# One block for the whole layer: rows normalised inside the attention, shared weights split in its last batch, first shared products in its last head

## The reference, cut to what matters

```
x                         (4, 1024, 512) float32: 4 batches of 1024 rows, width 512
qkv   = x @ w_qkv         16 heads of 128 for q, k and v
probs = softmax(q k^T / sqrt(128))
value = einsum('bhqk,bhkd->bhkd', probs, v)     # = v * (column sums of probs)
x     = layernorm(x + value @ w_o)
...
scores = sigmoid(x @ router_w.T); sc = scores + e_bias
# 8 groups of 4 experts, the 3 best groups by their two best, then the 4 best experts
w      = scores of those 4, normalised, x 2.5
# per expert 160 slots of ... tokens in order of arrival (capacity 1.25 * T * 4 / 32 = 640)
out[token] += w * (silu(x W_gate[e]) * (x W_up[e])) W_down[e]
shared = silu(x shared_gate.T) * (x shared_up.T) @ shared_down.T      # inner width 512
x      = layernorm(x + out + shared)
```

## Time and profile before

| what | value |
|---|---|
| median of 3 runs | 2881.0 us (2876.99 to 2883.53) |
| the profiled execution: its own time | 2872.05 us |
| its span in the trace | 2870.3 us |
| mean granted TensorE clock | 0.976 |
| PE busy | 2761.8 us, 96% |
| DVE busy | 2209.1 us, 77% |
| ACT, POOL busy | 1358.2 and 710.2 us, 47% and 25% |
| DMA | 203.14 MB, mean 71 GB/s |

### The profile page before, as it was taken

How to read it: one execution, slowest core, us unless ns; L and a number is a source line. 1 busy time by engine, 2 the same in 40 slices (tenths; PEclk the granted TensorE clock), 3 DMA queues, 4 the chain that set the end, 5 groups by cost and what they waited for, 6 DMA issues and landing times. The chain is left out here.

```text
span 2870.3 us, 42196 instructions
## 1 busy us (share of the span) xinstructions
PE 2761.8 (96%) x12832; PEld 2290.3 (80%) x12832; DVE 2209.1 (77%) x3407; ACT 1358.2 (47%) x2305; POOL 710.2 (25%) x623
## 2 busy tenths in 40 slices
PE   8999999999999999999999999999997888799998
PEld 6888888888888888888888888888875766688876
DVE  5888888888888888888888888888886876233346
ACT  4555555555555555555555555545542221144434
POOL 1122121222221121212121211111101355466620
PEclk9999999999999999999999999999997888899999
DMA  3111111121111111211111020110005430378953
GB/s 114 37 38 33 37 33 40 33 95 33 37 39 34 33 33 62 66 37 33 36 33 40 29 92 30 32 37 29 29 8 174 136 104 30 93 235 246 263 157 132
DMA packets 222007, 203.14 MB, mean 71 GB/s; under 512 B 18861, under 2 KB 170493, under 8 KB 221937
## 3 DMA queue, kind: packets, MB, share of 16 engines
q1 hardware_dynamic: 207600, 191.04, 20.9%
q0 software_dynamic: 14336, 11.23, 2.3%
HBM read 167.90 MB, written 44.21 MB: 74 GB/s over the span
## 5 line engine op out<-in xcount | busy, mean ns | idle before, releaser
L540 PE MATMUL p_g<-xt,w_sb 128*128 (+1 forms) x4608 | 1109.1, 390 | 9.6 <-DVE xt L505 9.6
L540 PEld LDWEIGHTS p_g<-xt,w_sb 128*128 128x128 f32 x4608 | 866.6, 188 | 190.3 <-DVE xt L505 10.2
L359 ACT ACTIVATE y_even<-p_s,neg_max 128x1024 f32<-128x1024 f32 x512 | 572.7, 1119 | 941.5 <-DVE neg_max L415 941.4
L415 DVE TENSOR_REDUCE neg_max<-p_s 128x1 f32<-128x1024 f32 x512 | 625.9, 1222 | 290.5 <-PE p_s L555 286.9
L555 PE MATMUL p_s<-qk 128*128 128x512 f32 x3072 | 781.0, 390 | 7.3 <-ACT y_even L359 7.3
L555 PEld LDWEIGHTS p_s<-qk 128*128 128x128 f32 x3072 | 576.9, 188 | 129.5 <-ACT y_even L359 6.5
L430 DVE SCALAR_TENSOR_TENSOR colsum<-y_even,inv,colsum 128x1024 f32<-128x1024 f32 x448 | 579.6, 1294 | 18.5
L265 POOL TENSOR_TENSOR w_sb<-w_raw,w_sb 128x512 fp32r<-128x512 f32 x192 | 257.0, 1339 | 1268.3 <-ACT w_sb L313 1268.3
L578 PE MATMUL p_o<-wo_sb,val 128*128 128x512 f32 x1536 | 374.0, 393 | 3.4 <-DVE val L458 3.2
L578 PEld LDWEIGHTS p_o<-wo_sb,val 128*128 128x128 f32 x1536 | 288.4, 189 | 69.5 <-DVE y_sb L465 5.4
L1722 PE MATMUL p_f<-x_parts,s_sb 128*128 128x512 f32 x768 | 196.3, 416 | 5.9 <-DVE arena L1490 3.4
(11 more groups left out here) (162 smaller groups left out, 2255.1 us busy)
## 6 DMA issues: line engine op xcount, KB each, us to landing
w_raw<-in_w_qkv SPq DMA_DIRECT2D x192, 256.0 KB, 2.9
wo_raw<-in_w_o SPq DMA_DIRECT2D x64, 256.0 KB, 2.8
y_sb<-in_x SPq DMA_DIRECT2D x32, 256.0 KB, 3.6
y_rows<-y_sb SPq DMA_DIRECT2D x32, 256.0 KB, 2.1
raw_own<-in_w_gate SPq DMA_DIRECT2D x16, 512.0 KB
raw_own<-in_w_up SPq DMA_DIRECT2D x16, 512.0 KB
raw_own<-in_w_down SPq DMA_DIRECT2D x16, 512.0 KB
arena<-in_w_gate SPq DMA_DIRECT2D x16, 512.0 KB
```

What stands on the lines that cost most here:

```text
L359: act.activation(ex[:, t % 2], p_s[:, t % 2], ACT.Exp, bias=neg_max[:, t % 2], accum_out=rowsum[:, t % 2]).then_inc(act_e, 1)
L415: dve.tensor_reduce(neg_max[:, t % 2], p_s[:, t % 2], AX_X, ALU.max, negate=True)\
L540: ins = pe.matmul(p_g[:, g % 2], w_sb[:, a, r, c], xt_part(batch_par, b, c, half * NB, NB), start=(c == 0 and (a, b) == PASSES[0]), stop=( ...
```

## The change

It puts both blocks into one (`layer`), with one PSUM tensor `banks` cut up for both stages and SBUF buffers used again (the shared gate and up weights `s_gu` lie in one half of the transposed x `xt`, the transposed turns `parts` in the other). The order that is written out in each engine's `pair` and behind it changes so:

- In batches 1, 2 and 3 (counted from 0) the rows of the batch before are normalised in place in `y_sb`: the first 512 in the second head of the batch's first pair, the others in the first head of its second (`finished`). DVE does the statistics (`read_x`, L1023) in tiles 1 to 4 and the scale (`scale_x`, L1026 to L1032) in tile 5, ACT writes in tiles 6 and 7, SP's `swap` moves to the second pair and stores to `x2` (and the odd turn to `acc`) in place of `y`. The first two pairs of every batch are unrolled for it on DVE, ACT, POOL and SP.
- In the last batch SP loads eight pieces of the shared gate and up weights where x pieces came before (`load_gu`); ACT and POOL split them as they did x.
- In the last head PE transposes turn 0 (rows read back from `x2`) and does 18 of the first 24 gate/up products; behind it gate/up groups of turn 0 stand between and around the last `spread` and the out tiles.
- Turns 0 to 5 are read back from `x2` normalised; only turns 6 and 7 are normalised behind the attention. The router's and the shared down weights are loaded once the last out tile is done, the bias, the constants and the empty table at the kernel's start.
- Three scatters are under way in place of two. `hot` is kept in bf16, `chosen` goes, and `count` sums the four choices on PE: 56 matmuls of 32 columns in place of 14.
- `down` does three of the four chunks for all four tiles, then the fourth for all; before, tiles 0 and 1 were finished before 2 and 3 began.
- Weights of experts 1 and 0 are loaded before the routing's turns 1 on, of 2 after the store of turn 4, of 3 after that of turn 7.

```
         def pair(i):                                    # DVE
...
                     if t >= 1:
                         add_tile(n, t - 1)
+                    if 1 <= t <= 5 and finished(i, s) is not None:
+                        if t <= TT:
+                            read_x(finished(i, s), t - 1)
+                        else:
+                            scale_x(finished(i, s))
+                    if is_last(i) and s == 1 and t in (1, 3):
+                        lo_t(0, t - 1)
+                        lo_t(0, t)
...
+    def finished(i, s):
+        if isinstance(i, int) and i >= PB and (i % PB, s) in ((0, 1), (1, 0)):
+            return 2 * (i // PB - 1) + i % PB
+        return None
...
         def pair(i):                                    # ACT
...
                     exp_tile(n, t)
+                    if t >= 6 and finished(i, s) is not None:
+                        write_x(finished(i, s), range(2 * t - 12, 2 * t - 10))
+                    if is_last(i) and s == 1 and t in (0, 2):
+                        hi_t(0, t)
+                        hi_t(0, t + 1)
...
         def pair(i):                                    # PE
...
+                    if is_last(i) and (s, t) in ((0, 7), (1, 1)):
+                        turn(0, 2 * s)
+                        turn(0, 2 * s + 1)
+                    if is_last(i) and s == 1 and 3 <= t <= 5:
+                        gate_up(0, 0, range(6 * (t - 3), 6 * (t - 2)))
...
         pair(PAIRS - 1)
+        gate_up(0, 0, range(18, 24))
+        gate_up(0, 1)
         pe.wait_ge(dve_y, T * (PAIRS - 1))
         spread(M - 1)
+        gate_up(0, 2)
         pe.wait_ge(dve_v, 2 * M)
         for j in range(T):
             if j in (4, 5):
                 pe.wait_ge(dve_y, T * (PAIRS - 1) + j - 1)
             out_tile(PAIRS, j)
+        gate_up(0, 3)
+        turn(1, 0)
+        turn(1, 1)
+        logits(0)
...
         def swap(b, s):                                 # SP
-            for j in range(4 * s, 4 * s + 4):
-                on_sp.wait_ge(dve_y, (b * PB - 1) * T + j + 1)
-                store_y(b - 1, j)
+            for j in range(TT * s, TT * s + TT):
+                on_sp.wait_ge(act_ln, T * (b - 1) + j + 1)
+                sp.dma_start(x2_rows[:, b - 1, j], y_sb[:, j]).then_inc(out_y[j], 16)
+                if s == 1:
+                    sp.dma_start(acc_rows[:, b - 1, j], y_sb[:, j]).then_inc(out_y[j], 16)
...
                 for k in range(TOPK):                   # POOL
-                    on_pool.wait_ge(out_t[k % 2], 16 * ((TT * TOPK * c + TOPK * j + k) // 2))
+                    i = (c * TT + j) * TOPK + k
+                    on_pool.wait_ge(out_t[i % UNDER_WAY], 16 * (i // UNDER_WAY))
...
         def weigh(c):                                   # DVE
...
-            for q in range(2):
-                on_dve.wait_ge(out_t[q], 16 * TT * TOPK // 2 * (c - 1))
+            for q in range(UNDER_WAY):
+                on_dve.wait_ge(out_t[q], 16 * scattered(q, TT * TOPK * max(c - 1, 0)))
...
-            ro.then(dve.tensor_reduce(chosen[:], hot[:].rearrange("p t k e -> p t e k"), AX_X, ALU.max))
...
         def count(c):                                   # PE
...
             for j in range(TT + 1):
                 to = p_c[:, j * E:j * E + E]
-                for i in range(min(j, TT)):
-                    ins = pe.matmul(to, every[:], chosen[:, i], start=(i == 0), stop=(j == TT and i == TT - 1))
-                if j < TT:
-                    ins = pe.matmul(to, before[:], chosen[:, j], start=(j == 0), stop=True)
+                terms = [(every, i, k) for i in range(min(j, TT)) for k in range(TOPK)]
+                if j < TT:
+                    terms += [(before, j, k) for k in range(TOPK)]
+                for n, (mask, i, k) in enumerate(terms):
+                    ins = pe.matmul(to, mask[:], hot[:, i, k], start=(n == 0), stop=(n == len(terms) - 1))
...
-        def down_first(n):
+        def down(n):
             if n == 0:
                 on_pe.wait_ge(pool_s, 2)
             on_pe.wait_ge(dve_h, IC * (n + 1) - 1)
-            down(0, range(IC - 1))
-            down(1, range(IC - 1))
-            on_pe.wait_ge(dve_h, IC * (n + 1))
-            down(0, [IC - 1])
-            down(1, [IC - 1])
-        def down_second():
-            down(2, range(IC))
-            down(3, range(IC))
+            for j in range(TT):
+                if j == 2:
+                    on_pe.wait_ge(dve_f, IC * (n + 1))
+                down_part(j, range(IC - 1))
+            on_pe.wait_ge(dve_h, IC * (n + 1))
+            for j in range(TT):
+                down_part(j, [IC - 1])
```

More of the change, by code:

```diff
@@ L735, in last_norm, with layer @@
 def last_norm(nc, acc, out):
-    norm1 = KEPT.pop()
-    with norm1.stack:
-        after_attention(nc, norm1, acc, out)
-def after_attention(nc, norm1, acc, out):
-    y, router_wT, e_bias, shared_w, x2, table = norm1.routing
-    weights, C_SLOTS = norm1.experts
-    N, D = y.shape
+    calls = KEPT.pop()
+    with calls.stack as ctx:
+        layer(nc, ctx, calls, acc, out)
+def layer(nc, ctx, calls, acc, out):
+    x, xT, w_qkv, w_o = calls.attention
+    router_wT, e_bias, shared_w, x2, table = calls.routing
+    weights, C_SLOTS = calls.experts
+    B, S, D = x.shape
+    DH = 128
+    H = w_o.shape[0] // DH
+    M = B * H
+    C = D // P
+    T = S // P
+    HALVES = S // NB
+    PAIRS = M // 2
+    PB = H // 2
+    SCALE = float(DH) ** -0.5
+    Q, K, V = range(3)
+    G = 3 * HALVES
+    assert T == 8 and HALVES == 2 and PB == T and C == 4
+    N = B * S
     E = router_wT.shape[1]
@@ L1873, in _ @@
[L1873 to L1878 removed]
+            for i in of:
+                r, k, (a, b) = i // (KC * len(PASSES)), i // len(PASSES) % KC, PASSES[i % len(PASSES)]
+                at = slice(r * I + f * P, r * I + f * P + P)
+                ins = pe.matmul(p_f(f % 2, r), s_gu[:, a, k, at], parts[:, PARTS_OF[u], b, k],
+                                start=(k == 0 and (a, b) == PASSES[0]),
+                                stop=(k == KC - 1 and (a, b) == PASSES[-1]))
@@ new lines, in _ @@
+        gate_up(3, 0)
+        count(5)
+        turn(7, 0)
+        turn(7, 1)
+        gate_up(3, 1)
+        turn(7, 2)
+        turn(7, 3)
+        gate_up(3, 2)
+        count(6)
+        logits(7)
+        gate_up(3, 3)
+        down(3)
+        gate_up(4, 0)
+        count(7)
+        for f in range(1, IC):
+            gate_up(4, f)
+        down(4)
+        on_pe.wait_ge(dve_e, TURNS)
+        transposes(0)
+        transposes(1)
+        expert_gate_up(0)
+        for e in range(E):
+            if e + 2 < E:
+                transposes(e + 2)
+            if e + 1 < E:
+                expert_gate_up(e + 1)
+            if e == E - 2:
+                turn(1, 0, True)
+                turn(1, 1, True)
+            if e == E - 1:
+                turn(1, 2, True)
+                turn(1, 3, True)
+            expert_down(e)
@@ L1882 @@
+        gate_up(5, 0)
+        turn(3, 0, True)
+        turn(3, 1, True)
+        gate_up(5, 1)
+        gate_up(5, 2)
+        turn(3, 2, True)
+        turn(3, 3, True)
+        gate_up(5, 3)
+        down(5)
+        gate_up(6, 0)
+        turn(5, 0, True)
+        turn(5, 1, True)
+        gate_up(6, 1)
+        gate_up(6, 2)
+        turn(5, 2, True)
+        turn(5, 3, True)
+        gate_up(6, 3)
+        down(6)
+        for f in range(IC):
+            gate_up(7, f)
+        down(7)
 N_EXPERTS_FACTOR = (5, 4)
```

2855 lines of the change are left out of this document (1367 added, 1488 removed).

## The result

The changed kernel took 2935.43 us (median of 4, 2930.76 to 2938.12) against 2879.99 of the kernel before: a ratio of 1.019, 95% interval 1.017 to 1.021. Slower by 55 us, where 2832 was forecast. The profiled execution spans 2936.4 us.

What follows compares the result with a forecast made beforehand. PE, busy 96% of the span, was taken as the bound, with the experts waiting behind the last scatter. 12 - 15.7 + 8 - 57 + 4 = -49 from 2872 gives 2823, plus 9: 2832 us, range 2805 to 2862.

Steps and rivals of the forecast that it cites:

- A: Attention, batches 2 to 4: normalising rows there makes DVE late at PE's out tiles, 4.1 us a batch, +12 us.
- B: Seam between attention and routing: turn 0's work fills PE's waits, first scatter at 2233 instead of 2248.71, -15.7 us.
- C: Routing's scatters: three under way, 1.28 us apart, 182 us in all instead of 239, -57 us.
- D: From the last scatter to the experts, 11.9 us before: same code, 0.
- E: Late part: `down`'s new chunk order makes DVE's additions begin 2.8 us later, two other downs 0.65 each, +4 us.
- Same code: 0: Last scatter to experts (11.9 us) and the experts' 253 us: taken as unchanged, since the code is the same.
- the routing must keep up: Routing: PE has some 177 us of work until 2430, scatters end at 2435; close, and scatters decide.
- R4: Routing, slower: PE at a low clock becomes the bound, 2898 us at clock 0.6; chance 0.05.
- The closing sentence of the prediction: Routing: the forecast is wrong if scatters wait for DVE turn by turn, since then the routing, not POOL, is the chain.
- The clock's +8: Seam: at clock 0.75, 48 us of work takes 16 more; 0 if filled waits lift the clock; half taken.
- R1: Scatters: the third slot buys nothing, pitch stays 1.42 us, +19 us, 2851 us; chance 0.20.
- The stalls that I kept for transfers: Scatters: about 7.5 MB of transfers left, at 2.5 us a MB, hold them up 19 us.

Runs made afterwards that it cites:

- e5: The changed kernel, unedited, measured again on another chip: 2877.87 us.
- e6: The changed kernel with the 64-byte tile `token` allocated ahead of `xt` instead of behind it: 2844.40 us, ratio to the kernel before 0.9877.
- e17: The changed kernel, unedited, again on a different chip, as marker of that job's chip: 2878.76 us.
- e7: e6 with `down` in its former order of tiles: 2837.24 us.
- e8: The kernel before with three scatters under way in place of two: 2865.65 us against 2876.70.
- e3: The kernel before with an unused 64-byte tile put behind `xt`: 2917.40 us against 2878.05.
- e1: The changed kernel with an unused 64-byte tile ahead of `ident`, moving `w_sb` away from `xt`: 2883.07 us.
- e12: e7 with a tile of 512 bytes ahead of `ident`, so that `w_sb` moves and `xt` stays: 2833.51 us (one run).
- e14: e7 with a tile of 256 bytes ahead of `ident`, on the chip with the slow stretches: 2906.16 us (one run).
- e13: The changed kernel, unedited, a third time, on a chip that showed the slow stretches: 2945.88 us.
- e11: The changed kernel, unedited, a second time, on a different chip: 2879.33 us.

## Why the prediction was wrong

The kernel came out slower where faster was forecast, and 73 us above the range's upper end. Point by point, by its own steps, in us against the kernel before (traces; the changed kernel in e5, so without the stretches, and the same with its buffers placed well, e6):

| step of the sum | forecast | measured |
|---|---|---|
| pitch of the matmuls | not seen | +38.8 (first scatter of e5 - e6) |
| A, normalisation in the attention | +12 | +22.8 (last `project`, e6) |
| B and clock, seam | -15.7 + 8 = -7.7 | -8.1 (first scatter +14.7, less 22.8) |
| C, scatters | -57 | -53.5 (185.6, not 239.1); +3.5 in the first measurement |
| D, to the first expert | 0 | -0.0 |
| experts | 0 | +6.0 (e5), -0.6 (e17), +2.6 in the first measurement |
| E, late part | +4 | +3.6 (e5), +7.7 (e17 and the first measurement), of it 2.9 behind the last matmul and 1.2 in two waits |

**The step that failed first is one that wasn't there.** "Same code: 0" was taken for granted of every instruction that the diff only moved to other buffers. I read the change as work that is added, removed or moved in time, and not as the new memory layout that comes with putting both blocks into one. Over the attention's 9472 matmuls the 39 us are 4.1 ns each, 4.6 in the steady windows. With the buffers placed well, on a chip without the stretches, the changed kernel takes 2844.40 (e6), within the stated range and 12 above the forecast.

**The second is C's clause "the routing must keep up".** It does, on three chips: with POOL waiting once. On the fourth and in the first measurement it doesn't, and that is the largest single miss: +3.5 us for the scatters where -57 was forecast. Not because DVE or PE have too much to do, the rival that I wrote as R4 (PE the bound, at a low clock, 2898): the clock did fall, to 0.80 and in the stretch to 0.59, but in e5, with the same work and no standstill, it is 1.00 in that stretch. The closing sentence of the prediction named the sign, scatters waiting for DVE turn by turn. What stands behind it, instructions that start late while scatters run, was nowhere among the rivals, and why they start late stays open.

**A was undersized.** The waits were found where forecast, at the out tiles, 1.0 and 3.7 us a batch (e6; 0.7 and 3.4 at the slower pitch of e5) where 1.2 and 2.9 stood: 14.1 us for 12. What was left out is what follows: after the longer wait PE's next 12 matmuls take 1.5 to 2.6 us more, at a lower clock, 5.7 us in all. The last 3 of the 22.8 aren't accounted for.

**B was right in its sum, and in its terms less so.** PE's first hold in the last head was 5.94 (6.4 forecast), the second 5.33 (2.7). The clock's +8 was half of a full term, taken because nothing decided between the two ends; in e6 the granted clock is 1.00 from 2190 to 2230 and 0.66 from 2230 to 2250, where it was 0.74 to 0.77 from 2180 to 2240 before. That the halves met at -8.1 is in part luck. (The lowest 20-us slice before was 0.74, not 0.75; it changes nothing.)

**C as a rate was right**: 1.27 apart, 184 to 186 us for all (182 forecast), so rival R1 is out. The stalls that I kept for transfers are there: 22.1 us of waiting for scatters in e5, where 19 were forecast. The Trainium skill ("DMA: Bandwidth & Descriptors", "Queues, rings and completion order") says that each DMA engine takes its queues in turn, packet by packet. That scatters would then hardly be held up was my inference from it, and the 22.1 us don't agree with the inference.

**D and E** came as forecast in what the change does: E with 2.9 us behind the last matmul (3 forecast) and two waits of 0.62 (0.65 each), all of which the former order of `down` takes back (e7). The rest of the late part isn't E's. A wait of PE ahead of turn 3's second transposes was 2.2 us in the kernel before, 2.7 in e5 and 5.0 in the first measurement, and with three scatters in the kernel before (e8) 6.9; so the +3.6 of e5 is a lucky agreement.

## What to carry to other kernels

A kernel that is laid out anew in memory is a new kernel for its matmuls: before any argument on order, count matmuls per 100 us in a stretch that hasn't changed, before and after, and if the pitch moved, move the buffers against each other until it is back. Here a tile of 64 bytes was enough, both to slow a kernel (e3) and to mend one (e6).

Time a kernel on more than one chip before a verdict of 2%. And a wait of PE costs more than itself: what it does for the next microseconds, at a lower clock, is part of the price.

## What the runs showed of the hardware that was not expected

- Where the buffers of the moving operand and of the weights of `project`'s matmuls (128x512, 4-byte operands) lie 64 or 128 bytes past a multiple of 2048 bytes from each other, the attention's matmuls start 230.7 to 231.3 ns apart on average (e1, e3, the changed kernel), at a distance of 0, 256 or 512 past it 226.8 (e6, e12, e14); the granted clock is 1.00 in both. The slower pace lasts for some 7 to 11 matmuls into groups whose own operands lie well.
- On one of five chips (e13 and e14; not in e1, e5, e11 and e17), and in the first measurement, while three scatters were kept under way and POOL issued one each 1.27 us, single instructions of PE came in steps of about 0.7 us and ACT didn't begin for up to 31.6 us with its inputs there. The stretches ended 2.0 to 4.1 us after the last scatter of a run. The cause is open.
- The third scatter under way brought single scatters from 1.5 us apart (medians of 1.50 to 1.54 with two) to 1.27, POOL's own 0.97 and 0.30 to the next.
